# A routed expert layer: keys split once and resident, keys as the moving operand, sums turned by TensorE, row transfers of two steps

## The chip, the cores and the metric
One core of a Trainium2 chip runs the whole program. The metric is the device time of one execution in microseconds. The kernel before takes 1265.13 us, the median of 3 runs (1262.3 to 1270.8).

## The reference
A layer over N = 8192 tokens (8 sequences of 1024) of width D = 256, in float32, in two parts. The first, here "mixing", is an attention-like block (four projections, a scan over time, an output projection, and a key-value mix of width 1024 with a gate). The second is a mixture of 32 experts, of which every token uses 4:

```python
gates = jax.nn.sigmoid(jnp.einsum('nd,ed->ne', xt, expert_sel))
sel_val, sel_idx = jax.lax.top_k(gates, N_HEADS)            # N_HEADS = 4
gate_full = jnp.zeros_like(gates).at[jnp.arange(N)[:, None], sel_idx].set(sel_val)
scores = jax.nn.relu(jnp.einsum('nd,edf->nef', xt, keys))   # keys: 32 x 256 x 128
scores = scores * gate_full[:, :, None]
out = jnp.einsum('nef,efv->nv', scores, values)             # values: 32 x 128 x 256
```

with xt the layer-normalised output of mixing, and `x + out` returned.

## The kernel before
**Stages.** Mixing runs over 16 tiles of 512 tokens, as a software pipeline of 19 steps. While it runs, tokens are routed: for each of a tile's 2048 (token, expert) pairs VectorE works out a row of `lists`, and GpSimd scatters the token's row there with 16 indirect DMAs per tile (L1312). `lists` in HBM consists of 288 units of 128 rows; all rows of one unit belong to one expert. A table `plan_expert` names each unit's expert. Units that fill first are handled first: the first 48 places in the order (the "head") hold units in an order of their own, so their rows are moved one unit at a time, at an address that is read from a table (`plan_row`, `plan_store`); the rest is in order of address.

**The expert stage** has 144 steps of two units (256 rows), each a chain over five engines. To keep float32 precision with fast products, every operand is split in a rounded part (hi, type fp32r) and what is left of it (lo), and a product is hi·hi + hi·lo + lo·hi. Step i:
- SyncE loads the rows of step i (L1466 in the head, two DMAs of 128 KB; L1470 else, one of 256 KB; 2 KB per partition) into one of 4 homes `xr`, after `x_ready` of step i-4.
- ScalarE reads the two experts from the table in registers (`experts_of`, L1416) and rounds their keys (L1585); VectorE, with registers of its own, forms the rest (L1645, one step later). The raw keys of all experts are resident in `experts_raw`; the split is made anew in every step.
- TensorE transposes the rows (L1531, 4 products with the identity) into PSUM; ScalarE rounds them (xt_hi, L1593), VectorE forms xt_lo (L1652).
- TensorE, two steps later: the inner product with the keys as the stationary and the rows as the moving operand, 6 products per unit of 128 columns each (L1543). The result has the hidden index on partitions, which the next product needs. ScalarE and VectorE form h_hi and h_lo with the relu (L1596, L1660).
- TensorE, four steps later (`Y_LAG`): h is stationary, the expert's values move, 3 products per unit of 256 columns (L1523 to L1525). ScalarE copies the result from PSUM (L1601) to one of 4 homes `y`, and one step later its queue stores it to `sorted_rows` (L1576, two DMAs of 128 KB in the head; L1579 one of 256 KB).

On each engine a step's instructions stand in a fixed order and wait on semaphores; the loops `Fori` take 16 steps per iteration, after 32 (TensorE, ScalarE) or 48 (VectorE, SyncE) steps written out.

**The sums.** For tile t GpSimd waits until the outputs of the first 8(t+3) steps are stored, then issues 16 indirect gathers (L1690), 4 for each group j of 128 tokens, each of 128 rows of 1 KB; `ye` holds 4 groups. VectorE adds them, times the gates, to the residual, two additions in each of its steps from step 34 on (L1634). SyncE loads the residual of a tile (L1481) and stores the finished tile (L1487, the last in four parts L1507).

**The start.** SyncE's first row load waits for `head_ready` and for the scatters of all tiles but the last. Values are split in eight parts of 4 experts: ScalarE rounds (L846), VectorE subtracts (L887), four parts before `plan_head`, the rest in the first steps. `plan_later` (L1231) and `plan_end` finish the table of experts.

## Time and profile before

| | |
|---|---|
| three runs | 1262.3, 1265.13, 1270.8 us |
| profiled execution | 1268.08 us, span 1266.3 us |
| mean granted TensorE clock | 0.955 of full |
| TensorE, VectorE, ScalarE, GpSimd busy | 91%, 83%, 63%, 61% of the span |
| instructions | 25326 |
| expert stage, by the first and last inner product | 816.5 to 1226.8 us |
| DMA, 40 slices | 0 to 4 tenths in mixing, 9 in the expert stage from 900 us on |
| chain that ended last | PE 27%, GpSimd 25%, VectorE 17%, issue 17% |

Times in the profile count from the start of the span. Busy shares of TensorE are of modelled, overlapping instructions. "PE" is TensorE, "PEld" its weight loads, "DVE" VectorE, "ACT" ScalarE, "POOL" GpSimd, "SP" SyncE; a q behind the name is the engine's queue (loads of registers, DMA issues). The mean duration of a product is longer than the distance between two of them, for they overlap; the distance is read from start times.

### The profile page before, as it was taken

What the parts mean: (1) busy time and instruction counts of PE and PEld (TensorE: products, weight loads), DVE (VectorE), ACT (ScalarE), POOL (GpSimd) and SP (SyncE); (2) the same over time, 40 slices, a digit from 0 to 9 for tenths busy, and PEclk for the clock granted to TensorE, in tenths of its full rate; (3) what the DMA queues carried; (4) which work ended last, traced back from release to release, by engine and by line L of the source; (5) the groups of instructions that cost most, each with busy time, mean ns of one, the idle gap of its engine ahead of it and who ended that gap; (6) DMA issues with size and microseconds to landing.
All of it is one profiled execution on the core that took longest, in us unless ns stands there. A gap on an engine that the chain in (4) does not pass through costs nothing.

```text
span 1266.3 us, 25326 instructions
## 1 busy us (share of the span) xinstructions
PE 1147.0 (91%) x7118; PEld 999.8 (79%) x7119; DVE 1053.8 (83%) x2397; ACT 801.7 (63%) x1633; POOL 773.9 (61%) x868
## 2 busy tenths in 40 slices
PE   7799999999999999999999996499999999999970
PEld 6678887787887787887887875399998998998970
DVE  4788899899899898899889977766888897888874
ACT  4467667568558557558557556277876776767650
POOL 2433368658558558658658666710567676675766
PEclk9799999999999999999999998599999999989895
DMA  9422134324314314314312137466999999999984
GB/s 344 149 84 100 60 108 144 104 86 147 120 64 153 133 45 145 139 47 157 133 47 87 59 129 295 140 200 198 301 316 332 313 311 324 310 296 313 315 281 142
DMA packets 131097, 227.07 MB, mean 179 GB/s; under 512 B 15584, under 2 KB 74976, under 8 KB 129632
## 3 DMA queue, kind: packets, MB, share of 16 engines
q1 hardware_dynamic: 82272, 121.49, 28.4%
q0 software_dynamic: 24576, 67.14, 17.0%
q10 hardware_dynamic: 24192, 37.76, 7.9%
q8 instruction: 26, 0.43, 0.1%
q14 instruction: 31, 0.25, 0.1%
HBM read 100.50 MB, written 125.83 MB: 179 GB/s over the span
## 4 chain that ended last, share of the span: by engine, by line
PE 27%; POOL 25%; DVE 17%; issue 17%; ACT 5%; DVEq 4%; DMA 2%; ACTq 2%; POOLq 1%; SPq 0%
POOL lists L1312 13%; PE ps L444 7%; PE ps L1543 7%; DVEq L1416 3%; DVE keys L1645 3%; PE ps L1531 2%; PE ps L1523 2%; POOL th_r L1355 2%; POOL rs L1266 2%; DVE resid L1634 2%; POOL xp L1342 2%; DVE xp L971 1%; PE ps L1524 1%; DVE stats L863 1%; DVE h_lo L1660 1%
## 5 line engine op out<-in xcount | busy, mean ns | idle before, releaser
L1690 POOL DMA_INDIRECT ye<-sorted_rows,place_of x256 | 257.9, 1007 | 174.4 <-DMA sorted_rows<-y 79.1
L1543 PE MATMUL ps<-xt_hi,keys 128*128 128x128 f32 x1152 | 229.0, 285 | 1.9 <-DVE keys L1645 1.8
L1543 PEld LDWEIGHTS ps<-xt_hi,keys 128*128 128x128 f32 x1152 | 193.2, 199 | 2.9 <-DVE keys L1645 2.9
L1312 POOL DMA_INDIRECT lists<-rows_even,slot x128 | 146.3, 1143 | 46.0 <-issue 40.3
L1634 DVE SCALAR_TENSOR_TENSOR resid<-ye,gates,resid 128x256 f32<-128x256 f32 x256 | 123.5, 482 | 56.2 <-issue 34.1
L1312 POOL DMA_INDIRECT lists<-rows_odd,slot x128 | 140.5, 1097 | 44.5 <-issue 40.3
L1543 PE MATMUL ps<-xt_lo,keys 128*128 128x128 f32 x576 | 162.4, 282 | 0.0
L1593 ACT ACTIVATE xt_hi<-ps 128x512 fp32r<-128x512 f32 x144 | 86.1, 598 | 113.6 <-PE ps L1543 95.7
L1013 DVE TENSOR_TENSOR k_lo<-ksq,k_hi 128x512 fp32r<-128x512 f32 x128 | 118.9, 947 | 17.2 <-ACT k_hi L770 17.0
L1652 DVE TENSOR_TENSOR xt_lo<-ps,xt_hi 128x512 fp32r<-128x512 f32 x144 | 99.0, 688 | 38.2 <-ACT xt_hi L1593 37.5
L1585 ACT ACTIVATE keys<-experts_raw 128x256 fp32r x288 | 104.8, 415 | 22.6 <-issue 20.1
L761 ACT ACTIVATE kr<-ps,bias_k 128x512 f32<-128x512 f32 x128 | 86.7, 683 | 47.2 <-PE ps L444 44.5
L1543 PEld LDWEIGHTS ps<-xt_lo,keys 128*128 128x128 f32 x576 | 114.6, 199 | 0.0
L1523 PE MATMUL ps<-values_hi,h_hi 128*128 x288 | 94.2, 327 | 22.4 <-DVE h_lo L1660 20.5
L444 PE MATMUL ps<-xn1t_hi,wt_hi 128*128 128x512 f32 x256 | 105.2, 411 | 6.2 <-DVE xn1t_lo L875 3.2
L1645 DVE TENSOR_TENSOR keys<-experts_raw,keys 128x256 fp32r<-128x256 f32 x288 | 108.4, 418 | 0.6 <-issue 0.2
L1058 DVE RECIPROCAL u<-u 128x512 f32<-128x512 f32 x32 | 106.8, 3337 | 0.0
L444 PE MATMUL ps<-xn2t_hi,wk_hi 128*128 128x512 f32 x256 | 103.9, 406 | 2.3 <-ACT kr L761 0.3
L651 PE MATMUL ps<-k_hi,wv_hi 128*128 128x512 f32 x256 | 103.2, 403 | 0.0
L444 PE MATMUL ps<-xn1t_lo,wt_hi 128*128 128x512 f32 x256 | 102.0, 399 | 0.0
L444 PE MATMUL ps<-xn1t_hi,wt_lo 128*128 128x512 f32 x256 | 101.9, 398 | 0.0
L444 PE MATMUL ps<-xn2t_hi,wk_lo 128*128 128x512 f32 x256 | 101.6, 397 | 0.0
(211 smaller groups left out, 3184.5 us busy)
## 6 DMA issues: line engine op xcount, KB each, us to landing
lists<-zeros SPq DMA_DIRECT2D x18, 2048.0 KB, 10.0
xr<-lists SPq DMA_DIRECT2D x120, 256.0 KB
sorted_rows<-y ACTq DMA_DIRECT2D x120, 256.0 KB
x_sb<-in_x SPq DMA_DIRECT2D x16, 512.0 KB, 3.9
residual<-xp SPq DMA_DIRECT2D x16, 512.0 KB, 4.6
experts_raw<-in_expert_in SPq DMA_DIRECT2D x8, 1024.0 KB, 15.5
resid<-residual SPq DMA_DIRECT2D x16, 512.0 KB, 5.9
out_dram<-resid SPq DMA_DIRECT2D x15, 512.0 KB, 5.9
```

The costliest lines, as they stand in the source:

```text
L444: mm = pe.matmul(bank, w(k), m(k), start=n == 0, stop=n == last)
L651: pe.matmul(bank, wv_hi[:, f, c], k_hi[:, f, :], start=f == 0, stop=False, skip_group_check=True)
L1013: dve.tensor_tensor(k_lo[:, m, :], ksq[:, m % KRING, :], k_hi[:, m, :].bitcast(F32), ALU.subtract).then_inc(klo_ready, 1)
L1058: dve.reciprocal(u[:, m, :], u[:, m, :]).then_inc(rden_ready, 1)
L1312: pool.indirect_dma_start(lists, bass.IndirectOffsetOnAxis(ap=slot[:, q, n:n + 1], axis=0), rows[q][:, n // TOPK, :], None).then_inc(last_ ...
L1523: pe.matmul(cols, h_hi[:, q % HS, c], v_hi, start=True, stop=False)
L1543: mm = pe.matmul(ps[:, H + q % HBANKS, s * P:(s + 1) * P], keys[:, q % SLOTS, s, half, k * DE:(k + 1) * DE], m[:, q % XTS, c], start=n == ...
L1585: ins = act.activation(keys[:, r % SLOTS, s, 0, :], raw_keys(e), ACT.Copy)
L1634: dve.scalar_tensor_tensor(acc, ye[:, j, k, :], gate, acc, ALU.mult, ALU.add).then_inc(sum_step, 1)
L1645: ins = dve.tensor_tensor(keys[:, q, s, 1, :], raw_keys(e), keys[:, q, s, 0, :].bitcast(F32), ALU.subtract)
L1652: dve.tensor_tensor(xt_lo[:, q], ps[:, XT + r % SLOTS, :], xt_hi[:, q].bitcast(F32), ALU.subtract).then_inc(x_ready, 1)
L1690: pool.indirect_dma_start(ye[:, j, k, :], None, sorted_rows[0:(tile + 3) * OPENED * UNIT, :], bass.IndirectOffsetOnAxis(ap=place_of[:, n:n ...
```

## The change
- **Keys.** All keys are split once, at the end of mixing, to a resident tile `keys[expert, k, hi|lo, 128]`; values to `values[expert, hi|lo, 256]`. ScalarE and VectorE no longer split keys in a step nor read experts from the table. The split runs in eight parts: keys before values (`round_keys`, `split_keys`), seven parts of keys before `plan_head`, the eighth and the values' parts in the first steps; `plan_later` moves from before step 0 to before step 3.
- **Inner product.** The rows become the stationary operand and the keys move: for each unit and half k of the width, one product of xt_hi with hi and lo keys side by side (256 columns), and one of xt_lo with the hi keys (128). The result has tokens on partitions; ScalarE copies the lo columns (`sums`), VectorE adds the hi columns, and TensorE transposes the sum (two products with the identity per step) before the relu.
- **Transfers.** Rows are loaded and outputs stored in batches of two steps, 512 KB, 4 KB per partition (in the head four DMAs of 128 KB). There are 3 homes of two steps for rows, 2 for outputs. A store is issued in every second step.
- **Lags.** Inner product 3 steps behind the transpose, the sum's transpose 5, the values' product 7 (were 2 and 4); sums on VectorE from step 36 (was 34). Residuals have 3 homes.
- **Loops.** 48 steps written out, then a loop of 48 steps per iteration. TensorE reads the experts of four steps at once (8 registers), once for the keys and once for the values. VectorE waits for TensorE's step at the head of its own.

The diff, cut to its core:

```diff
+WIDE = 2
+FOLD = WIDE * SUB
+H_LAG = WIDE + 1
+C_LAG, Y_LAG = H_LAG + 2, H_LAG + 4
+HOMES = (3, 2, 4, 2, 2, 3, 4)
+SUM_LAG = 36
+PLAN_STEP, FIRST_RESIDS, KEYS_FIRST = 3, 14, 7
...
+        keys = nc.alloc_sbuf_tensor_at("keys", [P, E, KD, 2, DE], F32R, offset=arena_at)
+        values = nc.alloc_sbuf_tensor_at("values", [P, E, 2, D], F32R, offset=arena_at + HALF)
...
             if last:
-                round_experts(0, ROUND_FIRST)
+                round_keys(0, LOADS)
...
             if last:
-                round_experts(ROUND_FIRST, LOADS)
+                round_values(0, 2)
...
+        def split_keys(dve, first, end):
+            for n in range(first, end):
+                dve.wait_ge(keys_rounded, n + 1)
+                for k in range(KD):
+                    ins = dve.tensor_tensor(keys[:, part(n), k, 1, :],
+                                            experts_raw[:, part(n), k * DE:(k + 1) * DE],
+                                            keys[:, part(n), k, 0, :].bitcast(F32), ALU.subtract)
+                ins.then_inc(keys_split, 1)
...
-                split_values(dve, 0, VALUES_FIRST)
+                split_keys(dve, 0, KEYS_FIRST)
                 plan_head()
...
@@ on_sync
+        def rows(b, r):
+            q = r % XB
+            if in_head(b):
+                for n, at in enumerate(held_rows(sp, plan_row, b * FOLD, LIST_ROWS - UNIT)):
+                    sp.dma_start(xr[n * PART_OF:(n + 1) * PART_OF, q],
+                                 lists[bass.ds(at, UNIT), :].rearrange("(p f) d -> p f d", f=FOLD)
+                                 ).then_inc(rows_loaded[q], 16)
+            else:
+                sp.dma_start(xr[:, q], lists[bass.ds(b * (FOLD * UNIT), FOLD * UNIT), :]
+                             .rearrange("(p f) d -> p f d", f=FOLD)).then_inc(rows_loaded[q], 16)
...
@@ on_tensor
+        def inner(i, r, pair):
+            b, q = i - H_LAG, r - H_LAG
+            experts = experts_of(b, q, "keys")
+            pe.wait_ge(x_ready, SPAN * pair + q // WIDE * WIDE + WIDE)
+            after(pe, sums_ready, b - 1)
+            for s, e in enumerate(experts):
+                cols = ps[:, AB + q % 2, s * 2 * DE:(s + 1) * 2 * DE]
+                for k in range(KD):
...
+                    pe.matmul(cols, xt_hi[:, home, c],
+                              keys[:, bass.ds(e, 1), k].rearrange("p a h w -> p (a h w)"),
+                              start=k == 0, stop=False, skip_group_check=True)
+                    mm = pe.matmul(cols[:, 0:DE], xt_lo[:, home, c],
+                                   keys[:, bass.ds(e, 1), k, 0].rearrange("p a w -> p (a w)"),
+                                   start=False, stop=k == KD - 1, skip_group_check=True)
+            return mm
...
+        def turn_sums(i, r):
+            b, q = i - C_LAG, r - C_LAG
+            pe.wait_ge(sums_ready, b + 1)
+            after(pe, h_ready, b - 1)
+            for s in range(SUB):
+                mm = pe.transpose(ps[:, HT + q % 2, s * P:(s + 1) * P], sums[:, q % SUMS, s * P:(s + 1) * P], ident)
...
@@ on_scalar
         def store(b, r):
-            q = r % YS
-            if in_head(b) and b % HELD == 0:
-                held[:] = held_rows(act, plan_store, b, LIST_ROWS - SUB * UNIT + 1)
-            act.wait_ge(ycopy_ready, b + 1)
+            q = r % YB
+            act.wait_ge(ycopy_ready, (b + 1) * WIDE)
             if in_head(b):
-                for s in range(SUB):
-                    act.dma_start(sorted_rows[bass.ds(held[b % HELD * SUB + s], UNIT, SUB), :], y[:, q, s, :]
+                for n, at in enumerate(held_rows(act, plan_store, b * FOLD, LIST_ROWS - FOLD * UNIT + FOLD - 1)):
+                    act.dma_start(sorted_rows[bass.ds(at, UNIT, FOLD), :], y[:, q, n, :]
                                   ).then_inc(y_stored[q], 16)
...
         def step(i, r, pair):
-            if within(i, 0, NSTEPS):
-                for s, e in enumerate(experts_of(act, i)):
-                    ins = act.activation(keys[:, r % SLOTS, s, 0, :], raw_keys(e), ACT.Copy)
-                ins.then_inc(keyhi_ready, 1)
...
+            if within(i, H_LAG, NSTEPS + H_LAG):
+                q = r - H_LAG
+                act.activation(sums[:, q % SUMS, :].rearrange("p (s w) -> p s w", s=SUB), halves(q)[:, 1],
+                               ACT.Copy).then_inc(low_ready, 1)
...
@@ on_vector
         def step(i, r, pair):
-            if within(i, K_LAG, NSTEPS + K_LAG):
-                b, q = i - K_LAG, (r - K_LAG) % SLOTS
-                if r == 0:
-                    experts[PAIR - 1] = experts_of(dve, b)
-                dve.wait_ge(keyhi_ready, b + 1)
-                for s, e in enumerate(experts[(r - K_LAG) % PAIR]):
-                    ins = dve.tensor_tensor(keys[:, q, s, 1, :], raw_keys(e), keys[:, q, s, 0, :].bitcast(F32),
-                                            ALU.subtract)
-                ins.then_inc(keylo_ready, 1)
+            if within(i, 0, NSTEPS + C_LAG):
+                dve.wait_ge(pe_step, i + 1)
             add(i, r, pair, 0)
+            if within(i, H_LAG, NSTEPS + H_LAG):
+                q = r - H_LAG
+                total = sums[:, q % SUMS, :].rearrange("p (s w) -> p s w", s=SUB)
+                dve.wait_ge(low_ready, i - H_LAG + 1)
+                dve.tensor_tensor(total, halves(q)[:, 0], total, ALU.add).then_inc(sums_ready, 1)
...
+        split_keys(dve, KEYS_FIRST, LOADS)
+        split_values(dve, 0, 1)
+        for i in range(SPAN):
+            if i == PLAN_STEP:
+                plan_later(dve)
+            if i == PLAN_STEP + 2:
                 plan_end(dve)
-            if i == RING:
+            step(i, i % SPAN, i // SPAN)
+            if i < 4:
+                split_values(dve, 2 * i + 1, min(2 * i + 3, LOADS))
+            if i == PLAN_STEP + 2:
                 places_sorted(dve)
```

## Rows read from the trace of the kernel before

**Rows 1.** Windows: us, PE, PEld, DVE, ACT, POOL busy (count), clock, DMA share, GB/s.
```profile
896.00:1216.00 320.00, 299.13 (x2416) 290.51 (x2415) 271.58 (x653) 226.53 (x552) 224.33 (x222) 0.97 0.96 314
```

**Rows 2.** Chain of waits within the expert stage: start us, us, what.
```profile
1010.09 0.77 DVE keys L1645 x2
...
1011.00 0.85 DVEq L1416
...
1012.87 0.75 DVE keys L1645 x2
```

**Rows 3.** Groups from 850 to 1200 us: busy us, mean ns, idle before.
```profile
L1690 POOL DMA_INDIRECT ye<-sorted_rows,place_of x214 | 216.8, 1013 | 156.2 <-DMA sorted_rows<-y 79.1 <-issue 61.6 <-DVE resid L1634 15.5
...
L1634 DVE SCALAR_TENSOR_TENSOR resid<-ye,gates,resid 128x256 f32<-128x256 f32 x202 | 97.4, 482 | 33.0 <-issue 31.6
...
L1645 DVE TENSOR_TENSOR keys<-experts_raw,keys 128x256 fp32r<-128x256 f32 x243 | 91.5, 418 | 0.6 <-issue 0.2
...
L1652 DVE TENSOR_TENSOR xt_lo<-ps,xt_hi 128x512 fp32r<-128x512 f32 x122 | 83.9, 688 | 25.6 <-ACT xt_hi L1593 24.9
...
L1660 DVE SCALAR_TENSOR_TENSOR h_lo<-ps,h_hi 128x256 fp32r<-128x256 f32 x122 | 51.1, 419 | 2.4 <-issue 1.8
```

**Rows 4.** GpSimd's timeline, gathers: start us, us, engine, line, what, idle before.
```profile
893.07 0.99 POOL L1690 DMA_INDIRECT ye<-sorted_rows,place_of  x1 [65.17 <-DMA sorted_rows<-y]
...
938.49 0.94 POOL L1690 DMA_INDIRECT ye<-sorted_rows,place_of  x1 [3.35 <-DVE resid L1634]
...
959.77 1.00 POOL L1690 DMA_INDIRECT ye<-sorted_rows,place_of  x1 [0.30 <-DMA sorted_rows<-y]
...
1239.98 1.12 POOL L1690 DMA_INDIRECT ye<-sorted_rows,place_of  x1 [0.30 <-issue]
...
1259.25 0.94 POOL L1690 DMA_INDIRECT ye<-sorted_rows,place_of  x1 [0.30 <-issue]
```

**Rows 5.** TensorE's timeline, one step at the full clock.
```profile
829.58 0.60 PE L1531 MATMUL ps<-consts,xr 128*128 128x128 f32 x4
829.94 0.31 PE L1543 MATMUL ps<-xt_hi,keys 128*128 128x128 f32 x1
...
831.31 0.33 PE L1523 MATMUL ps<-values_hi,h_hi 128*128 x1
...
832.06 0.60 PE L1531 MATMUL ps<-consts,xr 128*128 128x128 f32 x4
```

**Rows 6.** ScalarE's timeline; then lines 1444, 1576: ns min/median/max, first and last start.
```profile
860.13 0.86 ACTq L1576 DMA_DIRECT2D sorted_rows<-y  x2
861.03 0.60 ACT L1593 ACTIVATE xt_hi<-ps 128x512 fp32r<-128x512 f32 x1 [1.07 <-PE ps L1543]
...
861.79 0.60 ACT L1601 ACTIVATE y<-ps 128x512 f32<-128x512 f32 x1
...
L1444 ACTq TENSOR_LOAD <-plan_store x4: 551/551/554, 848.7 to 879.8; - x4
...
L1576 ACTq DMA_DIRECT2D sorted_rows<-y x38: 338/338/1027, 841.0 to 889.0; - x38
```

**Rows 7.** DMA: packets, MB, share: 1000 to 1100; 765 to 780; landing, 850 to 1200.
```profile
q10 hardware_dynamic: 5035, 9.17, 23.9%
...
q1 hardware_dynamic: 642, 4.61, 73.2%
...
resid<-residual SPq DMA_DIRECT2D x14, 512.0 KB, 5.9
```

**Rows 8.** SyncE's waits; line 887; VectorE's window of `plan_later`.
```profile
SPq L1491 <- DMA lists<-rows_even,slot: 23.4, 1, 23.4
...
L887 DVE TENSOR_TENSOR experts_lo<-experts_raw,values_hi x8: 1219/1220/1226, 788.4 to 818.1; 128x1024 fp32r<-128x1024 f32 x8
...
805.10:809.10 4.00, 3.71 (x11) 0.50 0.34 110
```

**Rows 9.** A window across a fall of the clock, columns as in the first group.
```profile
976.00:981.00 5.00, 3.44 (x20) 3.30 (x19) 3.98 (x11) 2.67 (x7) 3.81 (x4) 0.75 1.03 370
```

More of the change, by code:

```diff
@@ L882, in split @@
                               ALU.subtract).then_inc(split_lo, 1)
+        def split_keys(dve, first, end):
+            for n in range(first, end):
+                dve.wait_ge(keys_rounded, n + 1)
[4 more added lines that the diff above has]
+                ins.then_inc(keys_split, 1)
         def split_values(dve, first, end):
@@ L1408, in expert_phase @@
+    BATCHES = SPAN // WIDE
+    HEAD_BATCHES = HEAD_END // FOLD
     SUM_END = SUM_LAG + 2 * NT * J
+    HELD = 4
+    PART_OF = P // FOLD
+    assert NSTEPS % SPAN == 0 and SPAN % HELD == 0 and SPAN // RING % RESIDS == 0 and HEAD_END <= SUB * SPAN
+    assert all(BATCHES % homes == 0 and HEAD_BATCHES % homes == 0 for homes in (XB, YB))
     def within(i, first, end):
         return not isinstance(i, int) or first <= i < end
-    def experts_of(eng, b):
-        _, values = nc.values_load_multi_w_load_instructions(
-            plan_expert[0:1, bass.ds(b * SUB, SUB)], engines=(eng.engine,), min_val=0, max_val=E - 1,
-            skip_runtime_bounds_check_because="the plan writes all of the table, bounded, ahead of its semaphores")
-        return values
@@ L1421, in raw_keys, with in_head, landed, held_rows @@
-    def raw_keys(e):
-        return experts_raw[:, bass.ds(e, 1), 0:KD * DE].rearrange("p a w -> p (a w)")
-    def uses(r, pair, slots):
-        return (PAIR // slots) * pair + r // slots
+    def in_head(b):
+        return isinstance(b, int) and b < HEAD_BATCHES
+    def landed(r, pair, homes):
+        done = (BATCHES // homes) * pair + r // homes
+        head = HEAD_BATCHES // homes
+        return 16 * (done + (FOLD - 1) * (min(done, head) if isinstance(done, int) else head))
+    def held_rows(eng, table, first, last):
+        _, at = nc.values_load_multi_w_load_instructions(
+            table[0:1, first:first + FOLD], engines=(eng.engine,), min_val=0, max_val=last,
+            skip_runtime_bounds_check_because="the plan writes all of the table, bounded, ahead of head_ready")
+        return at
@@ L1432, in group @@
         tile = n // J
-        return 2 * J * pair + n, 2 * pair + tile, tile % 2, n % J, pair + tile // 2
-    HALF, HELD = P // SUB, 4
-    assert HEAD_END % (SUB * HELD) == 0
-    def in_head(i):
-        return isinstance(i, int) and i * SUB < HEAD_END
-    def held_rows(eng, table, i, last):
-        _, at = nc.values_load_multi_w_load_instructions(
-            table[0:1, i * SUB:(i + HELD) * SUB], engines=(eng.engine,), min_val=0, max_val=last,
-            skip_runtime_bounds_check_because="the plan writes all of the table, bounded, ahead of head_ready")
-        return at
@@ L1504, in on_sync @@
+        with sp.Fori(1, NSTEPS // SPAN) as pair:
+            for r in range(SPAN):
+                step(SPAN * pair + r, r, pair)
+        for i in range(NSTEPS, OUT_AT + (NT - 1) * RING):
+            step(i, i % SPAN, i // SPAN)
+        last = (NT - 1) % RESIDS
         for j in range(J):
-            G = 15 * J + j
+            G = (NT - 1) * J + j
             sp.wait_ge(sum_step, TOPK * (G + 1))
-            sp.dma_start(out[G * P:(G + 1) * P, :], resid[:, 1, j, :]).then_inc(out_stored[1], 16)
@@ new lines, in on_tensor, with experts_of @@
+        held = {}
+        def experts_of(b, r, use):
+            n = r % HELD
+            if n == 0 or (use, r) not in held:
+                _, found = nc.values_load_multi_w_load_instructions(
+                    plan_expert[0:1, bass.ds(b * SUB, (HELD - n) * SUB)], engines=(pe.engine,), min_val=0,
+                    max_val=E - 1,
+                    skip_runtime_bounds_check_because="the plan writes all of the table, bounded, ahead of its "
+                                                      "semaphores")
+                for m in range(HELD - n):
+                    held[use, r + m] = found[m * SUB:(m + 1) * SUB]
+            return held.pop((use, r))
@@ L1683, in on_gpsimd @@
         for tile in range(NT):
-            for q in range(YS):
-                pool.wait_ge(y_stored[q], landed((tile + 3) * RING, 0, YS))
+            batches = (tile + 3) * RING // WIDE
+            for q in range(YB):
+                pool.wait_ge(y_stored[q], landed(batches + YB - 1 - q, 0, YB))
             for j in range(J):
```

350 lines of the change are left out of this document (170 added, 180 removed).

## The prediction
> **What bounds the kernel now.** I read the windows by stage first [rows 1], then the chain of waits, the costliest groups of the expert stage, and last GpSimd's timeline. From 896 to 1216 us, the bulk of the experts, TensorE is busy 93%, VectorE 85%, ScalarE 71%, GpSimd 70%, and the DMA share is 0.96. No single number names the bound.
>
> The chain does. In that stretch it runs through VectorE: keys subtraction, a register load of experts (0.85 us on VectorE's queue), keys again [rows 2]; from 1010.09 to 1012.87 is one step, 2.78 us. By the groups [rows 3] a step's VectorE work is two keys subtractions (418 ns each), one xt_lo (688), one h_lo (419) and two sums (482), 2.91 us less their overlaps, plus what nothing hides of the load. The 122 subtractions of xt_lo in 350 us make 2.87 us per step, clock falls and loop boundaries included.
>
> Behind it stands GpSimd. It issues 256 row gathers, 16 for each of 16 tiles. The first starts at 893.07, tile 2's at 938.49, tile 3's at 959.77, tile 15's at 1239.98, the last at 1259.25 [rows 4]. The first fifteen tiles take 346.9 us, 23.1 each. But tile 2, in which GpSimd hardly waited, took 21.3, and tile 15 20.2. So GpSimd has 8% of slack: once gathers run, eight steps cannot be shorter than 21.3 us, 2.66 each. From the last gather's end to the span's end is 1266.3 - 1260.2 = 6.1 us.
>
> So the kernel's end is: start of the first gather (G0), sixteen tiles, 6.1 us.
>
> **The tiles.** What the change does to a step:
>
> TensorE: at the full clock four row transposes take 0.36 us (829.58 to 829.94), twelve keys products 1.37 (to 831.31), six values products 0.75 (to 832.06) [rows 5]: 2.48 us. A product of 128 columns is 0.114, one of 256 is 0.125. After: four of 256 and four of 128 columns for the keys 0.96, transposes 0.36, two transposes of sums 0.18, values 0.75: 2.25 us. Its register loads change from one per step, of two values, to two per four steps, of eight; such a load costs 0.55 us on ScalarE's queue [rows 6], so there are fewer.
>
> The width itself gains: the pass of the lo keys rides along for 0.01 us. The Trainium skill (TensorE: Matmul & The Clock Gate, Back-to-back issue gap) gives about 81 ns for a 128-column product with its weight load. By that the twelve would cost 0.97 us, and the change would save 0.15 where the rows give 0.41; the rows disagree, and I go by them. TensorE is the bound in neither case.
>
> VectorE loses two keys subtractions (0.69 us as spaced) and the load of experts, of which 0.39 us showed beside xt_lo; it gains one addition like h_lo (0.34). 2.78 - 0.69 - 0.39 + 0.34 = 2.04 us. ScalarE loses two roundings of keys and its load and gains one copy of half of xt_hi's size: 1.9 us with its store. All are under 2.66: engines no longer set the step. GpSimd does.
>
> Row transfers: a 2 KB packet costs 85 ns (23.9% of 16 engines' 100 us for 9.17 MB), an 8 KB packet 312 (73.2% of 15 us for 4.61 MB) [rows 7], so 4 KB cost 156 against 171: 128 of them per step over 16 engines give 0.12 us of DMA time per step. The step's DMA need is now 0.96 x 2.87 = 2.75 us by the share, after it 2.63, just under 2.66; its bounds are 2.63 and 2.75, and I take the lower, as latency, not engines, lets it grow. Homes hold now: rows 3 batches of two steps, outputs 2 batches; a 512 KB store has about 8 us before a gather wants it and 6.4 before its home is wanted (it is issued at the head of one step, and the copy that wants the home is the last of the next but one: 2 x 2.66 + 1.1), and the loads of 512 KB land in 5.9 [rows 7].
>
> So a tile costs 21.1 us: 14 of them at 21.1, between 20.2 (tile 15, nothing beside it) and 21.3 (tile 2), nearer to the one under load, and the last two at 20.3 as now. Sum 336.
>
> **The first gather.** It needs step 23's output stored. The stage's start: VectorE splits seven parts of keys, at the price of a part of values (1,220 ns) 8.5 us where four parts cost 4.6. From 788.4 that ends at 797, and SyncE's 23.4 us of waiting for GpSimd's scatter, which ends near 807 [rows 8], hide it. The first rows come in four transfers instead of two: +1.0. Then VectorE puts seven values parts (8.5 us) between steps 0 to 3, and 3.7 us of planning ahead of step 3 [rows 8]; TensorE waits for the plan at its step 4. Working the steps through by these rows at TensorE's half clock, and letting each wait for VectorE's step before, I get step 4 at 827.3, step 7 at 836, step 8's end at 841, and the first store at 842.8.
>
> From there ScalarE sets the pace, and this is the term that I think the change costs. Each head batch is four separate stores, after a wait for the batch's last copy and a register load that the same wait holds back. Before, two stores and two roundings of keys overlapped (the engine rounds while its queue issues), and TensorE hid it. Now, from [rows 6]: three activations until y is done 1.36 (861.03 to 862.39), the new copy 0.3; semaphore 0.1; load 0.55; four issues at 0.52 (0.86 for two, less one's 0.34), 2.08; then the second step's four activations, the last one's end overlapped, 1.5. That is 5.9 us per two steps, 2.95 each, against 2.6 now (38 stores, 19 steps, from 841.0 to 889.0) and 2.25 that TensorE could. Its bounds: 2.25 if the issues hide, 3.3 if one store per batch takes the slowest's 1.03. I take 2.95, worked from ScalarE's own rows. Store 11, the one needed, is issued at 842.8 + 11 x 5.9 + 2.6 = 910.3; it lands 3.7 us later, as the one issued at 889.0 + 0.34 did. G0 = 914, 21 us later than now. The outputs' longer lag (7 steps for 4) is within this.
>
> **The sum.** 914 + 336 + 6.1 = 1256; 2 us for three loop boundaries at which gathers may wait: a span of 1258. The profiled execution took 1268.08 for a span of 1266.3, so 1260; its time lies 3 us over the median of 1265.13. Forecast 1257 us, 0.6% less. The gain of the steps (2 us per tile) and of waits that vanish is nearly eaten by the later G0.
>
> **Rivals.**
> A, clearly faster. ScalarE's queue hides its issues, or the head runs at TensorE's 2.3: step 31 is 14 us earlier, G0 = 897 to 900. And gathers issue faster: 0.94 us at the end, 1.01 on average in the stretch [rows 3, 4]; GpSimd then has less of VectorE's traffic beside it, as the keys subtractions are gone. At 20.3 us a tile: 898 + 16 x 20.3 + 6.1 = 1229. For it stand tile 15 and the slack of two steps between engines. Against: the half-microsecond issue is seen on each store. The Trainium skill (SBUF — State Buffer, SBUF: two separate sides) says GpSimd's port pair is locked by a VectorE operation with two SBUF inputs; keys subtractions and sums have two, the operations that read PSUM one; by it all gathers but those beside sums would go to 0.94. No row here tells this apart. Chance 0.30, 1225 to 1245.
>
> B, slower. Stores bind. Only two homes for outputs, of 512 KB each, at a DMA share near 1: ScalarE's y copy waits for the store of two batches ago, TensorE for ScalarE, and the gather of the next tile for the last store. It decides from the point where such a store takes over 8 us to land. And TensorE, idle for over a microsecond at a time, falls to half its clock, as near 978, after 1.56 idle of 5 us [rows 9]; at 1.2 GHz a step is 4.5 us. Then a tile keeps its 23.1 us: 914 + 15 x 23.1 + 20.2 + 6.1 = 1287. For: share 0.96, TensorE idle 15% of a step and a quarter of one in the head. Against: bytes per step are the same, and 5.9 is under 6.4. Chance 0.22, 1270 to 1295.
>
> C, the change of packet size does nothing: a step needs 2.75 us of DMA, 22 per tile: 14 x 0.9 = +13, 1270. It lies inside "no change"; chance 0.13.
>
> My forecast, 1247 to 1265, has 0.35.
>
> **Numbers.** One per cent, about what a measurement here can tell from no change, is 1252.5 and 1277.8. Faster: A, and a quarter of mine: 0.38. Slower: most of B: 0.18. Same: 0.44. The range leaves out A's lowest 7 us and B's top 10: 1232 to 1285. Signs are mixed; the likeliest case alone has 1247 to 1265.
>
> **What would show it.** First gather at 914 (mine), under 900 (A). In 845 to 905, ScalarE's stores in groups of four, 5.9 us apart, TensorE busy under 80%. From 950 to 1200, gathers with 0.30 us before each and tiles of 21.1: then GpSimd is the bound, and VectorE waits for ye. Waits of gathers for stores, or half clock in more than three places: B. DMA share over 0.98 at equal GB/s: C. I am wrong in kind if VectorE still never waits for a gather.

## The result: 2.7% slower, outside the range

The changed kernel takes 1300.25 us (median of four runs, 1299.32 to 1301.1) against 1263.72 us beside it: a ratio of 1.027, 95% interval 1.0232 to 1.0308. The forecast was 1257, its range ended at 1285. The profiled execution took 1300.49 us for a span of 1298.6, 40.6 us over the forecast span of 1258; the mean clock was 0.941 (0.955 before).

Windows of the changed kernel [rows 1], same columns:
```profile
916.00:1236.00 320.00, 271.90 (x2147) 263.98 (x2147) 226.74 (x530) 176.35 (x431) 205.59 (x212) 0.93 0.88 301
```
Every engine is less busy than before, and so is the DMA. Nobody is the bound: engines wait for each other. The groups from 850 to 1236 us [rows 3] say for what:
```profile
L1758 POOL DMA_INDIRECT ye<-sorted_rows,place_of x212 | 205.7, 970 | 200.4 <-DMA sorted_rows<-y 105.8 <-issue 91.5 <-DVE resid L1707 3.0
L1567 PE MATMUL ps<-keys,xt_hi 128*128 x516 | 138.3, 345 | 61.2 <-DVE sums L1717 30.0 <-issue 16.5 <-DVE xt_lo L1720 14.5
...
L1707 DVE SCALAR_TENSOR_TENSOR resid<-ye,gates,resid 128x256 f32<-128x256 f32 x207 | 99.1, 479 | 84.8 <-DMA ye<-sorted_rows,place_of 46.7 <-PE ps L1609 34.7 <-issue 1.8
L1720 DVE TENSOR_TENSOR xt_lo<-ps,xt_hi 128x512 fp32r<-128x512 f32 x128 | 87.6, 684 | 0.7
```
VectorE's sums wait 46.7 us for gathers; before, their waits up to 1200 us were nearly all "issue" [rows 3]. TensorE then waits 30 us for VectorE.

GpSimd's timeline, the first gathers of tiles 0, 3, 5, 8 and 9 [rows 4]:
```profile
916.82 0.98 POOL L1758 DMA_INDIRECT ye<-sorted_rows,place_of  x1 [86.76 <-DMA sorted_rows<-y]
...
988.80 0.94 POOL L1758 DMA_INDIRECT ye<-sorted_rows,place_of  x1 [8.67 <-DMA sorted_rows<-y]
...
1034.30 1.20 POOL L1758 DMA_INDIRECT ye<-sorted_rows,place_of  x1 [3.15 <-issue]
...
1106.05 0.94 POOL L1758 DMA_INDIRECT ye<-sorted_rows,place_of  x1 [3.58 <-issue]
...
1136.25 0.94 POOL L1758 DMA_INDIRECT ye<-sorted_rows,place_of  x1 [10.11 <-DMA sorted_rows<-y]
```
Inside a tile the gathers follow each other at 0.30 us; ahead of a tile's first one GpSimd stands 0.7 to 4.5 us, and twice 9 to 10. ("issue" here is a wait for a store's semaphore that the profile doesn't attribute.) The fourteen tiles forecast at 21.1 us take 24.0: with tile 14 starting at 1252.58, (1252.58 - 916.82) / 14.

The chain of waits around tile 5's first sum [rows 2], from the landing of tile 4's first gathers on; the first sum of tile 4 is at 1021.30, and 1038.32 is the issue of tile 5's fourth gather:
```profile
1021.30 0.14 DVE resid L1707
...
1023.50 0.45 PE ps L1584 x4
...
1026.73 0.51 DMA sorted_rows<-y
...
1038.32 6.73 DMA ye<-sorted_rows,place_of
...
1045.20 0.14 DVE resid L1707
...
1045.60 0.43 DVE sums L1717
...
1046.27 0.58 PE ps L1567
...
1048.23 0.87 PE ps L1584 x4
```
VectorE stands at its first sum until the gather lands; its addition for the inner product is queued behind, TensorE waits for that (3.4 us), and when it resumes, four transposes take 0.87 us where the same chain has 0.45 a tile earlier: the granted clock was 0.50 from 1047 to 1049 us. The store that this tile's gathers waited for is the one of 1026.73. From its issue to the first gather are 7.6 us, to the sum 18.5.

A step of TensorE that waits for nothing, by its timeline:
```profile
1011.12 0.28 PE L1567 MATMUL ps<-keys,xt_hi 128*128 x1
...
1011.98 0.62 PE L1584 MATMUL ps<-consts,xr 128*128 128x128 f32 x4
...
1012.57 0.37 PE L1607 MATMUL ps<-values,h_hi 128*128 x1
...
1013.24 0.28 PE L1609 MATMUL ps<-values,h_lo 128*128 x1
```
It ends at 1013.24 + 0.12: 2.24 us. The steps are as fast as forecast; the extra time lies between them.

### The profile page after: what moved, and what is told of

Same layout as the page of the kernel before. It is cut to its first block, busy times and chain, and to the rows that moved or that the text cites. A ratio compares the mean times of both kernels' runs of the same rounds, so it can differ in the third digit from the quotient of the medians.

```text
span 1298.6 us, 23707 instructions
## 1 busy us (share of the span) xinstructions
PE 1121.5 (86%) x6830; PEld 972.1 (75%) x6831; DVE 1012.3 (78%) x2268; ACT 752.4 (58%) x1504; POOL 762.6 (59%) x868
## 4 chain that ended last, share of the span: by engine, by line
POOL 29%; PE 23%; issue 19%; DVE 11%; DMA 9%; ACT 7%; ACTq 2%; POOLq 1%; DVEq 0%; SPq 0%
POOL lists L1340 12%; PE ps L452 8%; POOL ye L1758 6%; DMA ye<-sorted_rows,place_of 6%; PE ps L1567 3%; POOL rs L1294 2%; POOL th_r L1383 2%; DMA sorted_rows<-y 2%; PE ps L1584 2%; POOL xp L1370 2%; DVE xp L998 1%; ACTq L1648 1%; DVE stats L880 1%; ACT xt_hi L1666 1%; PE ps L1607 1%
## 5 line engine op out<-in xcount | busy, mean ns | idle before, releaser
L1758 POOL DMA_INDIRECT ye<-sorted_rows,place_of x256 | 247.6, 967 | 214.9 <-DMA sorted_rows<-y 105.8
L1567 PE MATMUL ps<-keys,xt_hi 128*128 x576 | 157.0, 349 | 69.0 <-DVE sums L1717 33.0
L1567 PEld LDWEIGHTS ps<-keys,xt_hi 128*128 128x128 f32 x576 | 116.8, 203 | 79.9 <-issue 79.6
L1663 ACT ACTIVATE sums<-ps 128x256 f32<-128x256 f32 x144 | 55.6, 386 | 196.6 <-PE ps L1609 163.4
L1570 PE MATMUL ps<-keys,xt_lo 128*128 x576 | 133.3, 231 | 0.0
L1570 PEld LDWEIGHTS ps<-keys,xt_lo 128*128 128x128 f32 x576 | 118.5, 206 | 0.0
L1584 PE MATMUL ps<-consts,xr 128*128 128x128 f32 x576 | 97.0, 295 | 12.0 <-DMA xr<-lists 12.0
L452 PE MATMUL ps<-xn2t_lo,wk_hi 128*128 128x512 f32 x256 | 101.3, 396 | 0.0
L1717 DVE TENSOR_TENSOR sums<-ps,sums 128x256 f32<-128x256 f32 x144 | 60.3, 419 | 51.9 <-ACT sums L1663 47.8
```

What stands on the lines that cost most here:

```text
L452: mm = pe.matmul(bank, w(k), m(k), start=n == 0, stop=n == last)
L1567: pe.matmul(cols, xt_hi[:, home, c], keys[:, bass.ds(e, 1), k].rearrange("p a h w -> p (a h w)"), start=k == 0, stop=False, skip_group_che ...
L1570: mm = pe.matmul(cols[:, 0:DE], xt_lo[:, home, c], keys[:, bass.ds(e, 1), k, 0].rearrange("p a w -> p (a w)"), start=False, stop=k == KD - ...
L1584: mm = pe.transpose(into.rearrange("p (t f) -> p f t", f=FOLD)[:, f, :], xr[:, b % XB, f, k * P:(k + 1) * P], ident)
L1758: pool.indirect_dma_start(ye[:, j, k, :], None, sorted_rows[0:(tile + 3) * OPENED * UNIT, :], bass.IndirectOffsetOnAxis(ap=place_of[:, n:n ...
```

## The experiments

All times are medians; a ratio is to the kernel before, run beside it. Theories: **1**, the sums come too late: between the last store that a tile's gathers need and VectorE's first sum of the tile lie a fixed number of steps (the *room*, 5 here). Steps got shorter; the *way*, from the issue of that store over the gathers to the data that the sum adds, did not. **2**, stores of 512 KB into two homes bind (rival B). **3**, the entry of the 48-step loop and its jump back cost time. **4**, ScalarE's stores pace the head.

**First four, one edit each from the changed kernel.**

`lag40`:
```diff
-SUM_LAG = 36
+SUM_LAG = 40
-RESID_AT = OUT_AT - 20
+RESID_AT = 31
```


> The sums start four steps later (from step 40), nothing else. Theory 1 (late gathers): from the issue of the store that a tile's gathers wait for to VectorE's first sum of that tile there are now 5 steps of TensorE, 11.3 us, while the way takes 17 us (store 5.6, semaphore 0.5, four gathers 4.5, landing 6.3); VectorE waits the 5.7 us in its fixed order and everything behind it, so a tile costs 18 + 5.7 = 23.7. Four more steps are 9 us: the wait goes, VectorE waits for gathers under 10 us in all (50.6 now), and the 13 tiles without a loop boundary fall from 22.9 to GpSimd's 21.3: 1280, or 1268 if the slack takes in the loop boundaries too. Theory 2 (stores of 512 KB into two homes bind): no change, 1297 to 1303. Theory 3 (loop boundaries are all of it): no change either.

Measured: 1284.63 us, ratio 1.0149 (1.0098 to 1.0200). Waits from 916 to 1250 us:
```profile
DVE resid L1707 <- PE ps L1609: 66.9, 39, 10.5
...
POOL ye L1758 <- DMA sorted_rows<-y: 21.0, 10, 4.1
...
PE ps L1584 <- DMA xr<-lists: 9.0, 6, 3.3
...
DVE resid L1707 <- DMA ye<-sorted_rows,place_of: 3.9, 2, 2.0
```
VectorE's waits for gathers fall from 50.6 to 3.9 us (the last row), and 1.2% of time is won: theory 1 is one cause. But the fourteen tiles without the jump back still take 22.3 us on average, and new waits stand there: VectorE for TensorE, GpSimd for stores, TensorE for rows. The last of them is in part the work of this edit, as `wide_lag40_noloop` below shows. The chain of waits has a store that landed late:
```profile
1055.99 10.45 DMA sorted_rows<-y
```

`noloop`, on all four engines:
```diff
-        with pe.Fori(1, NSTEPS // SPAN) as pair:
-            for r in range(SPAN):
-                step(SPAN * pair + r, r, pair)
+        for i in range(SPAN, NSTEPS):
+            step(i, i % SPAN, i // SPAN)
```


> All 144 steps written out on the four engines, so that there is no jump; nothing else. TensorE stands still for 8 and 9 us at steps 48 and 96, where the loop begins and jumps back. Theory 3 (fetching code after a jump costs 6 to 7 us each time, and the gathers then wait for a late store): the tiles 28.5 and 30.2 long become 23.5, 1288. Rival: the stalls at these steps are the late gathers again and stay, or straight code is fetched no faster: 1300.

Measured: 1291.16 us, ratio 1.0201 (1.0157 to 1.0244), 0.7% won, though the interval still touches the changed kernel's; tile 8 takes 24.85 us instead of 30.20, tile 2 only 27.1 instead of 28.5. Theory 3 holds for the jump back. The stall at the entry was mostly the late gathers: in `lag40`, which keeps the loop, tile 2 takes 21.7.

`narrow`:
```diff
-WIDE = 2
+WIDE = 1
-HOMES = (3, 2, 4, 2, 2, 3, 4)
+HOMES = (6, 4, 4, 2, 2, 3, 4)
...
                 pe.wait_ge(values_split, LOADS)
+                pe.wait_ge(plan_ready, 1)
```


> Transfers of one step (256 KB, 2 KB per partition, six homes for rows and four for outputs, the same bytes as now); lags 2, 4 and 6 follow from it. Theory 1: the store is issued with 6 steps of room (13.5 us) and lands in about 4 instead of 5.6, so VectorE's wait falls from 5.7 to about 2 per tile: 1255 to 1270, with the first gather some 5 us earlier. Theory 2 (the wide stores themselves bind): the same time, but VectorE's wait for gathers goes wholly, and no wait of ScalarE for its stores is left (9.6 us now). If width does nothing: 1300.

Measured: 1268.99 us, ratio 1.0023 (1.0001 to 1.0045): 2.5% won by undoing the width and the step of lag that goes with it (`H_LAG` is `WIDE + 1`), by which the room is 6 steps again. VectorE's waits for gathers fall from 50.6 to 31.8 us. First gather at 917.61, not 5 us earlier. Tiles take 20.1 to 22.2 us, except the one across the jump back:
```profile
1087.04 0.58 PE L1567 MATMUL ps<-keys,xt_hi 128*128 x1 [5.99 <-issue]
```
That tile has 27.76.

`headload`:
```diff
-            act.wait_ge(ycopy_ready, (b + 1) * WIDE)
             if in_head(b):
-                for n, at in enumerate(held_rows(act, plan_store, ...)):
+                at_rows = held_rows(act, plan_store, ...)
+            act.wait_ge(ycopy_ready, (b + 1) * WIDE)
+            if in_head(b):
+                for n, at in enumerate(at_rows):
```


> In the head ScalarE reads the rows of a batch's four stores before it waits for the batch's copies, not behind the wait. Theory 4 (ScalarE's queue paces the head, 5.9 us per batch, 0.55 of it the load): the first gather comes 12 x 0.5 = 6 us sooner, 911, and the time is 1294. Rival: the head is paced by something else, first gather at 917, 1300.

Measured: 1294.68 us, 1.0187 (1.0134 to 1.0240); first gather at 915.67, 1 us sooner, not 6. The interval overlaps the changed kernel's: inconclusive in time. The load was not what paced the head with four stores.

**Second four.**

`lag40_y3`, `lag40` and
```diff
-HOMES = (3, 2, 4, 2, 2, 3, 4)
+HOMES = (3, 3, 4, 2, 2, 2, 4)
```
(the third home lies where a residual's was, with `y` and `xr` moved in memory; ScalarE's first copy then has to wait for the last scatter, and the residuals' loads move to step 39)

> The sums start at step 40 and outputs have a third home of two steps (the memory comes from a residual's home: two instead of three). With the later sums alone fourteen tiles without a jump take 22.3 us on average, and a store of 512 KB now lands in up to 10.5 us where GpSimd gathers without a break; TensorE then waits for ScalarE's copy and that for the home. Theory 2 (once the late gathers are mended, two homes of 512 KB bind): ScalarE's waits for stores (9 us) go and these tiles fall to 21.0 to 21.3, 15 to 18 us less than with two homes, ratio to before 1.001 to 1.004. Rival (the remaining gaps are GpSimd waiting for the stores themselves, whose landing a third home doesn't shorten): ratio 1.015 as with the later sums alone.

Measured: 1285.31 us, 1.0138 (1.0111 to 1.0165): nothing won over two homes. Against theory 2 stands also that ScalarE's copies wait only 9.6 us in all for a home in the changed kernel. What waits now, from 916 to 1240 us:
```profile
POOL ye L1761 <- DVE resid L1710: 45.2, 23, 9.3
...
PE ps L1585 <- DMA xr<-lists: 12.6, 8, 3.6
```

`spstore`, head stores from SyncE's step 14 + 2b:
```diff
+                    sp.wait_ge(ycopy_ready, (b + 1) * WIDE)
+                    for n, at in enumerate(held_rows(sp, plan_store, b * FOLD, ...)):
+                        sp.dma_start(sorted_rows[bass.ds(at, UNIT, FOLD), :], y[:, b % YB, n, :]
+                                     ).then_inc(y_stored[b % YB], 16)
```


> The head's stores, four for each batch of two steps with their table's load, are issued by SyncE instead of ScalarE, at the same place in time. Theory 4 (ScalarE's four issues pace the head at 5.9 us per batch): ScalarE's 3 us gap per batch goes, TensorE runs at 2.3 us per step, and by step 23 of the outputs 9 to 12 us are won, first gather at 905 to 908; the tiles stay 23.7, so 1288 to 1291. Rival: SyncE's row loads come late behind the stores (4 loads and 4 stores at 0.45 us and two table loads are 4.7 us per batch) and the head keeps its pace, 917 and 1300.

Measured: 1294.96 us, 1.0216 (1.0192 to 1.0241); first gather at 913.62. From 886 us on a step takes 2.3 us on average (twelve copies of `y` in 27 us), as theory 4 says, but before that SyncE issues its row loads between the stores, and ScalarE's copy waits for its home (838 to 880 us):
```profile
ACT y L1680 <- DMA sorted_rows<-y: 10.3, 3, 6.1
```
Moving the four stores to the other queue moved the wait as well.

`planfirst`:
```diff
-PLAN_STEP, FIRST_RESIDS, KEYS_FIRST = 3, 14, 7
+PLAN_STEP, FIRST_RESIDS, KEYS_FIRST = 0, 14, 7
-        split_values(dve, 0, 1)
+        split_values(dve, 0, 3)
```


> Only the start: VectorE works out the plan for the later steps before step 0 (as in the kernel before) instead of before step 3, and three parts of values instead of one before step 0, in the 6.2 us in which it waits for the first rows. TensorE's 5.7 us stop ahead of its fourth step's products goes: values' product of step 0 at 832 instead of 837.4, first gather at 911, 1294 to 1295. Rival: VectorE's first xt_lo is late by as much as was moved ahead of it, first gather at 917, 1300.

Measured: 1305.26 us, 1.0294 (1.0239 to 1.0348); first gather at 920.38. A miss with a clear reason, in SyncE's and TensorE's waits:
```profile
SPq L1457 <- DMA lists<-rows_odd,slot: 8.5, 1, 8.5
...
PE ps L1584 <- DMA xr<-lists: 5.0, 1, 5.0
```
Rows of step 8 must not be loaded before the last tile's scatters have landed; that is GpSimd's time (835.2 in this run, 831.5 in the changed kernel, where SyncE waited 2.0 us). The products of values did begin earlier, at 833.1 instead of 837.8, but then the rows ran out. Part of the start is not VectorE's to give.

`narrow_noloop`, both edits above together:

> Transfers of one step, and all steps written out. With loops, transfers of one step left one tile of 27.8 us, at the jump back at step 96, and none at the loop's entry. Theory 3 (a jump costs TensorE 6 to 7 us, as it waits for code): that tile becomes 21.3, ratio to before 0.996 to 0.998 where it is 1.002 with the jump. Rival: straight code costs as much spread over the steps, 1.002.

Measured: 1261.69 us, 0.9944 (0.9917 to 0.9972); the tile across step 96 takes 22.23 instead of 27.76, and the intervals of the two ratios lie apart. This is theory 3 by itself.

**Third four.**

`before_lag32`, the kernel before with
```diff
-STORE_LAG, SUM_LAG = 7, 34
+STORE_LAG, SUM_LAG = 7, 32
```


> The kernel before, with its sums two steps earlier (from step 32 instead of 34). Theory 1 (room, counted in steps, between a tile's last store and its first sum): before has 6 steps of 2.78 us, 16.7, for a way of some 15.5 us (store of 256 KB 3.9, semaphore 0.5, four gathers 5, landing 6), and hardly waits. With 4 steps, 11.1 us, VectorE stands about 4 us in each tile and the loop closes as in the changed kernel: tiles of 25.5 to 26 instead of 23.1, 1295 to 1310, VectorE's waits for gathers over 40 us (12.5 now). Rival (the changed kernel's late gathers are a symptom of its stores or loops, and before has slack): under 1272.

Measured: 1306.99 us, 1.0299 (1.0257 to 1.0341). One number makes the kernel before as slow as the changed one: tiles of 26.1 us. The first gather of tile 1 by GpSimd's timeline, and the window from 936 us:
```profile
920.51 1.26 POOL L1690 DMA_INDIRECT ye<-sorted_rows,place_of  x1 [4.84 <-DMA sorted_rows<-y]
```
```profile
936.00:1236.00 300.00, 273.04 (x2001) 267.16 (x2001) 226.28 (x542) 184.86 (x455) 181.91 (x181) 0.87 0.88 277
```
The same picture: all engines less busy, DMA share 0.88, clock down, GpSimd waiting for stores. The way of tile 6, from the store that it needs to its first sum (ScalarE's and VectorE's timelines):
```profile
1047.70 0.35 ACTq L1579 DMA_DIRECT2D sorted_rows<-y  x1
...
1062.50 0.48 DVE L1634 SCALAR_TENSOR_TENSOR resid<-ye,gates,resid 128x256 f32<-128x256 f32 x1 [2.53 <-DMA ye<-sorted_rows,place_of]
```
14.8 us; with the four steps outside the room, 4 x 2.78 = 11.1, that is 25.9, and the tiles take 26.1 on average (this one 26.8). Only VectorE's waits for gathers stayed below what was expected, at 27 us. This is theory 1, made in a kernel that has neither wide transfers nor the long loop.

`halfstore`, rows loaded by two steps, outputs stored by one:
```diff
-    y = sb("y", [P, YB, FOLD, D])
+    YS = YB * WIDE
+    y = sb("y", [P, YS, SUB, D])
...
+                act.dma_start(sorted_rows[bass.ds(batch * (FOLD * UNIT), FOLD * UNIT), :]
+                              .rearrange("(p f) d -> p f d", f=FOLD)[:, half * SUB:(half + 1) * SUB, :], y[:, q]
```


> The changed kernel, but each step's outputs are stored by themselves (256 KB, four homes of a step instead of two of two steps, two stores per step in the head); rows are still loaded 512 KB at a time, lags as in the changed kernel. It parts the widths: if the stores' width is what transfers of one step mended (the way is 1.6 us shorter, the homes come free earlier, the head's four issues are spread), 1275 to 1283. If the row loads' width was it: 1296 to 1302. If both widths mattered little and the one step less of lag did it: 1290 to 1296.

Measured: 1286.74 us, 1.0130 (1.0084 to 1.0176). Of the 13 us between the profiled executions, 10 lie in the head: first gather at 906.67. The edit does two things there: two stores per step instead of four per batch, and the table's load ahead of the wait. Neither alone does it (`narrow` has the first, with a first gather at 917.6, `headload` the second, with 915.7). The fourteen tiles hardly move, 23.8 us after 24.0.

`narrow_held`, `narrow_noloop` and
```diff
-            act.wait_ge(ycopy_ready, (b + 1) * WIDE)
-            if in_head(b):
-                for n, at in enumerate(held_rows(act, plan_store, b * FOLD, ...)):
+            if in_head(b) and b % HELD == 0:
+                at_rows[:] = held_rows(act, plan_store, b * FOLD, ..., HELD * FOLD)
+            act.wait_ge(ycopy_ready, (b + 1) * WIDE)
+            if in_head(b):
+                for n, at in enumerate(at_rows[b % HELD * FOLD:(b % HELD + 1) * FOLD]):
```


> Transfers of one step, all steps written out, and ScalarE reads the head's store rows of four steps at once, ahead of the wait (as before). Theory 4 (ScalarE's queue paces the head; with one-step transfers 1.6 us per step behind the wait, 0.6 of it the table's load): a step of the head falls from 3.2 to 2.7 us, first gather at 905 to 908 instead of 917.6, and the time to 1250, ratio to before 0.985 to 0.988. Rival (the head is paced by the rows of step 8, which are not loaded before GpSimd's last scatter has landed at 831, and by SyncE): first gather at 915 or later, 0.993.

Measured: 1251.64 us, 0.9860 (0.9813 to 0.9907); first gather at 904.40, 13 us sooner, with a head step of 2.7 to 3.0 us instead of 3.2. Theory 4 holds: with two stores per step, what the load adds behind the wait is on the path.

`narrow_lag38`, `narrow_noloop` with `SUM_LAG = 38`, `RESID_AT = 31`:

> Transfers of one step, all steps written out, and sums two steps later (38). Theory 1: VectorE's 18 us of waits for gathers go and the tiles fall from 21.2 to 20.6: ratio 0.987 to 0.990. Rival (gathers then wait for the sums that free their homes, 11 us now): no gain, 0.994.

Measured: 1255.54 us, 0.9893 (0.9851 to 0.9934). Tiles 20.8 us, and between 828 and 1210 us the clock never falls. VectorE still waits 36.7 us for gathers (18.3 were there before the edit), but GpSimd no longer stands ahead of a tile: from tile 2 on its idle time there is the 0.30 us of every gather. The expected sign was wrong, the time right.

**Last four.**

`wide_lag40_noloop`, `noloop` and `lag40` together:

> The changed kernel with sums from step 40 and all steps written out: of the three differences to the version with one-step transfers, written-out steps and sums at 38 (0.989 of before, tiles of 20.8, no half clock), only the width and what goes with it is left. If late sums and jumps were all that held the tiles, 20.8 here too: first gather at 914, ratio 0.989 to 0.993. If wide transfers bind by themselves (rows and homes come late, up to 10 us a store): tiles of 22 on average, ratio 1.005 to 1.010.

Measured: 1277.76 us, 1.0066 (1.0033 to 1.0099); tiles 20.5 to 25.2, 22.4 on average, 1.7% over `narrow_lag38`. Waits of TensorE and of SyncE's queue, 916 to 1230 us, and the chain ahead of one of TensorE's:
```profile
PE ps L1583 <- DMA xr<-lists: 19.9, 8, 4.0
```
```profile
SPq L1489 <- DMA out_dram<-resid: 73.0, 12, 8.8
```
```profile
1114.11 7.39 DMA out_dram<-resid
...
1121.51 0.33 SPq L1489
...
1121.88 9.17 DMA xr<-lists
...
1131.09 1.03 PE ps L1583 x4
```
It is tempting to put the 1.7% down to the width, but this is a side effect of the edit to `RESID_AT`. L1489 loads a residual into the home of the tile three before it, and so waits until that tile's result has left it. In the changed kernel SyncE comes to this load 4 steps after it issued the store (30 + 24 - 50), in `narrow_lag38` 3 steps, here one (31 + 24 - 54). So SyncE stands there 12 times, up to 8.8 us, and the rows' load stands behind it in the same queue and lands late. `lag40` and `lag40_y3` have the same stand (73.4 and 75.3 us), the changed kernel none, `narrow_lag38` 6.4 us; and among the changed kernel's versions TensorE waits for rows in this stretch only in those with this edit or with step 39. What the width costs by itself can't be read from them.

`halfstore_lag40`, `halfstore` with the edits of `lag40`:

> Stores of one step, rows of two, sums from step 40, loops kept. With both wide and sums at 40 the ratio was 1.015. If the wide stores were the rest: tiles of 21.2, the head 8 us shorter as seen with these stores, ratio 1.000 to 1.004. If the wide row loads are the rest (TensorE waits for rows 9 to 13 us in all with sums at 40): only the head's 8 us, ratio 1.007 to 1.011, and TensorE still waits for rows.

Measured: 1285.41 us, 1.0112 (1.0076 to 1.0149), which the interval doesn't tell from `halfstore` nor from `lag40`. Narrower stores win nothing in the tiles; whether the row loads are late by their width stays open, since `RESID_AT` is 31 here too.

`before_lag36`, the kernel before with its sums at 36:

> The kernel before with its sums two steps later. If its 34 was just enough (16.7 us of room), nothing is won: VectorE's own 2.78 us per step and GpSimd's waits for sums remain, ratio 0.995 to 1.003. If late gathers cost it too, the tiles fall from 23.1 to 22.3: ratio 0.990.

Measured: 1261.63 us, 0.9929 (0.9896 to 0.9962): between the two cases expected; its fourteen tiles take 22.7 us for 23.3. The kernel before stood just at its edge.

`best`, `narrow_held` with `SUM_LAG = 38`, `RESID_AT = 31`:

> What the runs so far point to, together: keys resident and moving, transfers of one step, all steps written out, ScalarE's table read for four steps at once ahead of the wait, sums from step 38. First gather at 904.4, tiles as with sums at 38 (312 us for fifteen), the last 19.7, then 6: a span of 1242, ratio to before 0.979 to 0.982. Rival: with the earlier first gather the tiles lengthen, as TensorE and not GpSimd is then next: 0.986.

Measured: 1244.48 us, 0.9786 (0.9728 to 0.9843), faster than both kernels. Its window, and its groups from 850 to 1190 us:
```profile
936.00:1196.00 260.00, 241.56 (x2019) 231.25 (x2018) 220.20 (x511) 166.44 (x407) 198.72 (x202) 0.99 1.00 355
```
```profile
L1759 POOL DMA_INDIRECT ye<-sorted_rows,place_of x221 | 218.8, 990 | 142.4 <-DMA sorted_rows<-y 77.7 <-issue 58.2 <-DVE resid L1709 6.4
...
L1709 DVE SCALAR_TENSOR_TENSOR resid<-ye,gates,resid 128x256 f32<-128x256 f32 x213 | 102.2, 480 | 36.6 <-DMA ye<-sorted_rows,place_of 20.1 <-PE ps L1608 14.9 <-issue 1.4
```
First gather at 903.69, fifteen tiles of 20.7 us. GpSimd's idle time is 0.30 us per gather, which the profile calls issue; the DMA share is 1.00 at 355 GB/s. Here at last GpSimd is the bound that the prediction named, or the DMA queues beside it: with both full, no run tells them apart.

## Why the prediction was wrong

**The first gather: right.** Forecast 914, measured 916.82. The head's 48 stores are issued from 843.7 (842.8 forecast for the first) to 914.1, in groups of four 6.1 us apart (5.9). ScalarE's timeline shows the gap:
```profile
868.58 1.91 ACTq L1648 DMA_DIRECT2D sorted_rows<-y  x4
870.54 0.38 ACT L1663 ACTIVATE sums<-ps 128x256 f32<-128x256 f32 x1 [2.45 <-issue]
...
874.21 2.37 ACTq L1648 DMA_DIRECT2D sorted_rows<-y  x4
876.63 0.38 ACT L1663 ACTIVATE sums<-ps 128x256 f32<-128x256 f32 x1 [2.92 <-issue]
```
`halfstore` and `narrow_held` confirm it from the other side: they ease this queue, and the first gather comes 10 and 13 us sooner. Within it the part of the load was too large for four stores (`headload` won 1 us of 6).

**The step: right.** TensorE 2.25 forecast, 2.24 measured. Inside, the four pairs of keys' products took 0.86 us (1011.12 to 1011.98) where rows gave 0.96. The Trainium skill (TensorE: Matmul & The Clock Gate, Back-to-back issue gap) has some 81 ns for 128 columns with their load; an estimate by that page, with 0.125 from the rows for the 256 columns, is 4 x (0.125 + 0.081) = 0.82 us. The trace lies nearer to the page than to my rows; it changes nothing in the sum, since the rest of the step took the difference.

**DMA need: right in sign, and small.** From 1000 to 1080 us the changed kernel's stores:
```profile
q10 hardware_dynamic: 1872, 6.82, 21.2%
```
Counted as the prediction counts, by bytes, 6.82 MB are 1665 packets of 4 KB, and one costs 0.212 x 16 x 80 / 1665 = 163 ns, 156 forecast. (The count 1872 has smaller ones in it; so has the 5035 of [rows 7].) Per MB that is 5% less than before, where 9% was forecast.

**The tiles: the step that failed.** "GpSimd does [set the step]": 21.1 forecast, 24.0 measured. The fourteen tiles are 40.4 of the 40.6 us by which the span is longer than forecast. I compared what each engine needs per step and called the rest slack; a 512 KB store had "about 8 us before a gather wants it", with no working, and what follows the landing was left at nothing. But a tile is also a closed loop: store, gather, first sum, and from there in VectorE's fixed order the products of the steps whose outputs the next tile waits for. Its length is the way plus what it takes from the first sum to the next tile's store. By the rows above: first gather of tile 4 to its first sum, 1010.73 to 1021.30, 10.6 us; to the store for tile 5, 1026.73, 5.4; to the first gather of tile 5, 1034.30, 7.6; together 23.6. The granted clock was 1.00 from 1010 to 1034, so the loop takes this long without any fall of it; with one, in the next round, the middle part takes 7.0 us (1045.20 to 1052.21). The store goes out in step 8t + 31 and the first sum stands in step 8t + 36, a room of 5 steps, 5 x 2.25 = 11.3 us, for a way of 18.5. Before, the room was 6 steps of 2.78, 16.7 us. I listed three steps of lag added and two of SUM_LAG, and never set this room against the way. `before_lag32` closes the same loop in the other kernel, and its sum comes out too.

**Rival B came nearest in time, for the wrong reason.** It had 1287 and stores that land after more than 8 us. Its price, a tile that keeps 23.1 us, and its half clock were there. But the stores land in 5.7 us in the median and 8.3 at most, copies wait 9.6 us in all for a home, a third home won nothing (beside SyncE's stand), and narrower stores changed only the head.

**The sum of the causes**, each from ratios: the jump 0.7% (0.8% with narrow transfers), late sums 1.2%, with SyncE's stand against it (0.5% with narrow transfers, where the intervals overlap), the width with its step of lag 2.5% (2.6% with all steps written out). They overlap and don't add up, for the narrow kernels have a step more room: part of what undoing the width wins is theory 1. Without all three (`narrow_lag38`) the kernel stands at 0.9893, 1250 to 1256 us, with a first gather at 916 and tiles of 20.8: the forecast's 914 and 21.1. Its mechanism holds where the three are taken away; none of them was in its sum, but for 2 us of jumps. Its floor of 21.3 us for a tile was read too high, as `best` has tiles of 20.1 to 21.7. The "wrong in kind if VectorE never waits for a gather" was the wrong test: it waited, 50.6 us in the changed kernel with GpSimd idle between tiles, and 36.6 in `best`, where GpSimd has no gap between tiles. The wait is there in both cases and tells neither.

**Rival A** had its early first gather (897 to 900) at most at 903.69, in `best`. **C** fell with the share of 0.88.

What stays open: how the width's 2.5% divides between the step of lag that goes with it, the landing of stores and rows, and the head. Not tried were wide transfers with sums at 38 or 40 and the residual's load left 4 steps behind the store, narrow row loads with wide stores, and a fourth home for wide rows.

## What to carry to other kernels

Where one engine's fixed order ties a consumer to a producer several steps back, write the room in microseconds: steps times the *new* step, against the whole way (store, semaphore, issue, landing). A change that shortens the step shortens every such room, so lags have to grow with it. Lower busy shares on all engines and on the DMA together were the mark of such a closed loop here, in two kernels, and moving one lag by two steps in the *unchanged* kernel tests it in one run. When you move a lag, move all that hangs on it, and look at the waits of the queues too: one transfer that waits for its home holds up everything issued behind it.

## What was not expected of the hardware

- At the jump back over a 48-step body TensorE stops ("issue") 6.6 us in the changed kernel and 6.0 in `narrow`, and 5.2 to 9.5 in the other runs with it; in the changed kernel the granted clock was 0.76 from 1097 to 1110 us. In the kernel before, with loops of 16 steps, it has no such stop of 1 us or more from 850 to 1225 us. Written out, the longest ahead of an inner product was 0.6 us (`noloop`, 916 to 1250). What TensorE waits for there, no row shows.
- Under load (930 to 1210 us) the median landing of rows and stores of 256 KB was 4.4 to 5.8 us, that of 512 KB 5.3 to 6.9, so half the size saves little of the landing; the 5.9 that I took for 512 KB lay within the medians and said nothing of single ones of 9 to 10 us.
- Stores of 128 KB cost their queue about 0.5 us each (four in 1.83 to 3.25 us, the two shown in 1.91 and 2.37). With four per batch and the load behind the wait ScalarE's gap was 2.45 to 2.92 us, with two per step 1.6 (`narrow`), and with the load ahead of the wait besides 1.0 to 1.1, with a few of 1.3 to 1.8 (`best`).
- A gather took 0.97 us on average where VectorE's keys subtractions were gone, 1.01 before. The Trainium skill (SBUF — State Buffer, SBUF: two separate sides) has VectorE's operations with two SBUF inputs lock GpSimd's ports. The trace agrees in sign: in the changed kernel up to 1235 us, 51 gathers with no sum of VectorE's beside them took 0.95 us on average and 160 with one 0.98, and in `best`, with VectorE busier, all take 0.99.
